# The thirty middle batches of a cross-attention kernel: code written out thirty times, or one body in a run-time loop

## The reference

```python
qn, kvn = layer_norm(q, g_q, b_q), layer_norm(kv, g_kv, b_kv)
Q, K, V = heads(qn @ Wq), heads(kvn @ Wk), heads(kvn @ Wv)      # 16 heads x 32
scores = einsum('bhqd,bhkd->bhqk', Q, K) / sqrt(32)
attn   = softmax(scores, axis=-1)
ctx    = einsum('bhqk,bhkd->bhqd', attn, V).reshape(B, N_q, 512)
out    = q + gelu(ctx @ Wo + bo)
```

## Time and profile before

| | |
|---|---|
| median of 3 runs | 3265.35 us (3262.8 to 3265.62) |
| the profiled execution's own time | 3262.8 us |
| its span, first to last instruction | 3261.0 us |
| PE busy | 3230.8 us, 99% of the span, 16611 matmuls |
| DVE, ACT, POOL busy | 69%, 70%, 71% |
| DMA | 343 MB, mean 105 GB/s |

### The profile page before, as it was taken

The page is one execution under the profiler, slowest core; times in us unless marked ns, Lnnn a source line. Parts: engine busy times, 40 slices in busy tenths (PEclk is TensorE's granted clock), DMA queues, the critical chain, the costliest instruction groups (busy, mean ns, idle before and its releaser), DMA issues.

```text
span 3261.0 us, 49855 instructions
## 1 busy us (share of the span) xinstructions
PE 3230.8 (99%) x16611; PEld 2135.1 (65%) x16611; DVE 2256.9 (69%) x4769; ACT 2280.3 (70%) x3985; POOL 2313.9 (71%) x1544
## 2 busy tenths in 40 slices
PE   8999999999999999999999999999999999999998
PEld 5566666666666666666666666666666666666664
DVE  6667667676676676666766766766667767667664
ACT  5677666777767777667767667776777676677765
POOL 3676776777677767777776677777767776777765
PEclk9999999999999999999999999999999999999999
DMA  5655656566556656565665566665656655666653
GB/s 142 87 108 107 108 104 116 91 111 107 107 104 104 111 107 107 104 118 89 111 109 106 105 102 111 109 104 104 120 86 112 107 107 107 100 111 108 105 79 76
DMA packets 186721, 343.02 MB, mean 105 GB/s; under 512 B 20561, under 2 KB 20577, under 8 KB 186466
## 3 DMA queue, kind: packets, MB, share of 16 engines
q1 hardware_dynamic: 186000, 339.03, 60.0%
q10 hardware_dynamic: 466, 0.80, 0.2%
HBM read 104.87 MB, written 33.55 MB: 42 GB/s over the span
## 4 chain that ended last, share of the span: by engine, by line
PE 97%; DVE 1%; ACT 1%; issue 1%; DMA 0%; POOL 0%; SPq 0%; ACTq 0%; POOLq 0%; DVEq 0%
PE gen L856 43%; PE score L883 16%; PE score L876 15%; PE ctx L903 14%; PE gen L847 4%; PE gen L943 4%; PE gen L965 1%; DVE maxes L706 1%; DMA k_stack<-k_nat 0%; ACT q_stack L617 0%; PE score L788 0%; ACT probs L563 0%; DVE stats L725 0%; PE gen L837 0%; POOL probs L475 0%
## 5 line engine op out<-in xcount | busy, mean ns | idle before, releaser
L475 POOL TENSOR_TENSOR probs<-probs 128x1024 f32<-128x1024 f32 x762 | 1800.3, 2392 | 287.8 <-PE ctx L903 281.6
L706 DVE TENSOR_REDUCE maxes<-score 128x1 f32<-128x512 f32 x2048 | 1294.9, 680 | 217.5 <-PE score L883 213.9
L563 ACT ACTIVATE probs<-score 128x512 f32<-128x512 f32 x2048 | 1090.2, 621 | 141.1 <-PE score L876 137.5
L883 PE MATMUL score<-k_stack,q_stack 96*128 96x512 f32 x2048 | 761.2, 413 | 3.3 <-DVE maxes L706 1.8
L876 PE MATMUL score<-q_stack,k_stack 128*128 128x512 f32 x2048 | 696.4, 406 | 6.6 <-ACT q_stack L617 6.5
L883 PEld LDWEIGHTS score<-k_stack,q_stack 96*128 96x128 f32 x2048 | 378.2, 188 | 221.3 <-ACT probs L563 83.6
L876 PEld LDWEIGHTS score<-q_stack,k_stack 128*128 128x128 f32 x2048 | 374.7, 188 | 199.9 <-DVE maxes L706 64.4
L903 PE MATMUL ctx<-probs,v_sb 128*32 128x512 f32 x4096 | 492.5, 598 | 0.0
L856 PE MATMUL gen<-cT,w_k 128*128 128x512 f32 x1536 | 461.7, 400 | 0.2 <-DVE q_nat L688 0.2
L856 PE MATMUL gen<-w_v,cT 128*128 128x512 f32 x1536 | 461.4, 395 | 0.0
L856 PE MATMUL gen<-xT,w_q 128*128 128x512 f32 x1536 | 447.9, 394 | 0.0
(11 more groups left out here) (89 smaller groups left out, 2765.4 us busy)
## 6 DMA issues: line engine op xcount, KB each, us to landing
k_stack<-k_nat SPq DMA_DIRECT2D x384, 256.0 KB, 7.6
q_stack<-q_nat SPq DMA_DIRECT2D x381, 256.0 KB, 5.6
tok<-in_x SPq DMA_DIRECT2D x132, 256.0 KB, 11.0
tok<-in_ctx SPq DMA_DIRECT2D x128, 256.0 KB, 12.0
res<-in_x SPq DMA_DIRECT2D x124, 256.0 KB, 2.7
out<-res SPq DMA_DIRECT2D x124, 256.0 KB, 2.1
probs<-in_L_xattn_Wq SPq DMA_DIRECT2D x1, 1024.0 KB, 8.2
probs<-in_L_xattn_Wk SPq DMA_DIRECT2D x1, 1024.0 KB, 10.4
```

The source lines that it names most:

```text
L475: pool.tensor_tensor(probs[:, c + 1, heads], probs[:, c + 1, heads], probs[:, c, heads], ALU.add).then_inc(pool_added, 1)
L563: act.activation(probs[:, n, part, :], score_at(s, "st", i)[:], ACT.Exp, scale=SCALE).then_inc(exp_done, 1)
L706: dve.tensor_reduce(maxes[:, u1 % 2, SROW + i:SROW + i + 1], score_at(s, "s", i)[:], AX_X, ALU.max, negate=True).then_inc(max_done, 1)
L883: pe.matmul(score_bank(pe, b, s, "s", i)[:, :], q_stack[0:KROWS, u1 % 2, n, P * part:P * (part + 1)], k_stack[0:KROWS, u1 % 2, n, :], star ...
```

## The change

`all_batches` is called once for each engine. The Python loop over the 30 middle batches, which wrote each batch's instructions out, becomes a loop that the engine executes: `eng.Fori(1, B - 1)` yields a value held in a register of that engine, and `batch(b)` is built once with it.

```diff
             batch(-1)
             batch(0)
-            for b in range(1, B - 1):
+            with eng.Fori(1, B - 1) as b:
                 batch(b)
             batch(B - 1)
             batch(B)
```

## The result

The changed kernel takes 3281.31 us, the median of 4 runs (3277.87 to 3283.67), against 3265.12 us (3262.8 to 3265.62, 4 runs) for the kernel before: a ratio of 1.0051, with a 95% interval of 1.0039 to 1.0063. It is slower by 16 us, where 161 us were forecast. What happened is rival 2, for which 3276 us had been worked out. (The profiled execution of the kernel before, 3262.8 us, is one of the runs counted, not a further one.)

A forecast was written before the change was run, and what follows sets the result against it. PE was taken as the bound, with no idle time to win. Jump stalls 107, lowered clock 49 and register instructions 4.5 made 161 us, giving 3426 us; the forecast's own range was 3390 to 3465, the stated range 3272 to 3462.

The forecast's parts named there:

- rival 2: PE's jump: the loop's beginning is still in PE's instruction memory; 3276 us, up to 3305; chance 0.21.
- What bounds the kernel: Middle batches: PE is busy 99% with no idle time to win; its sequencer's lead is nothing behind each step's transpose.
- I take it that the beginning must be fetched again, with PE waiting: PE's jump back: the body's first packet is refetched; PE idles 3.7 us at each of 29 jumps, 107 us.
- The price of a fetch: PE's jump: one fetch takes 3.5 us, 2.3 for the smallest load plus 1.2 for the packet; bounds 0 and 5.6.
- The clock after the stall: PE behind each jump: granted clock drops for 3.5 us, losing 1.7 us; 49 us over 29 jumps.
- The control instructions: PE's jump: register addition, branch and fused instruction add 0.2 us each time.
- Register instructions elsewhere: PE behind the three other transposes of a batch: one uncovered 51 ns instruction each, 4.5 us in all.
- The other engines' jumps: ACT, DVE, POOL, SP: fetches of 2.8 us are hidden, counted 0; 0.5 us per jump, 15 us, if cover is gone.
- the first: PE's jump: the fetch stalls PE but the clock does not fall; 3377 us, or 3342 with the lowest fetch; chance 0.15.
- The third: PE's jump: code is kept and the 0.2 us per jump is regained by earlier transposes; 3266 us, chance 0.12.
- The fourth: PE's body: kept code saves 4 fetches a batch, each costing 0.2 us unseen; faster, 3251 us, chance 0.05.

The follow-up runs named there:

- with the hint: Changed kernel with PE's loop body holding two batches, plus a compiler branch prefetch hint naming the back edge's target at the body's start: 3288.52 us, ratio 1.0082.

## Why the prediction was wrong

The measured time lies inside the range of 3272 to 3462 us only because the range was stretched to take in rival 2; the forecast itself, 3426 with 3390 to 3465, missed. (Those two ends are somewhat wider than a fetch of 2.5 to 4.5 us gives with the prediction's own terms, 3397 and 3455.)

- **What bounds the kernel** held: PE has nothing to win, and its sequencer has no lead behind the transpose. That the jump stands at such a place is the reason why it costs anything; eighteen matmuls later it costs nothing.
- **"I take it that the beginning must be fetched again, with PE waiting"** is the step that failed: 107 of the 161 us, and with them the 49 of the clock; the runs show no fetch at a jump, and 0.33 us in place of the 3.7 us of idle time. From the earlier trace rows it was right that packets come one at a time as the program is passed. It does not follow that what is passed is gone: a body of 1157 instructions is kept, with 13 packets in the whole run, and one of 2294 is not. The experiments with two batches to a pass show both sides. The profile before could not tell: a stream of new code fetches one packet per 256 instructions whatever the memory holds. That reason should have stopped me from giving this case 0.47.
- (The Trainium skill, "Runtime: NRT & Kernel Launch", section on instruction fetch mechanics, was used for the forecast with its two-page window. The runs decide against it: a jump back over 4.5 packets found its target. Its other number, 2048 instructions for PE, lies between the two bodies tried. Its 512 for the other engines do not say when a body is kept: 496 on ACT were not.)
- **The price of a fetch**, 3.5 us, was too low where there is one: 8.6 us, of which some 6 pass before the packet starts. I had taken the idle machine's load; the upper end that I named, 5.6 us, was passed as well.
- **The clock after the stall** went with the stall: it stayed 1.00. The step itself holds where the stall is made: PE's gaps of 8.5 to 8.8 us brought the lower level all 14 times, gaps of 3.2 to 3.8 us in 27 of 28 cases, those of 2.8 and 2.9 us (with the hint) not. But 2.9 to 6.1 us at the lower level behind the long stalls are more than the 3.5 that I took.
- **The control instructions**, 0.2 us, were 0.33 at each jump: 9.7 us in place of 5.8. The branch alone takes 0.21 us, where I had argued from a semaphore wait of 0.05. (The Trainium skill, "Advanced Engine Details and Errata", control flow timing, has 108 ns for a compare-and-branch. By their records PE's takes 208 ns and ACT's 45, and to the next instruction it is about 260 on both; neither agrees.)
- **Register instructions elsewhere**: 4.5 us forecast, 6.8 found, and at another place. I looked only behind the transposes on PE; the run with the late waits put back says that it comes from the wait that a register instruction carries on DVE and ACT, on the way from the transpose to the next `st`. An engine that is busy for 69% of its time can still be on PE's path at one instruction.
- **The other engines' jumps**, counted at 0, cost 0, as the run with PE written out shows. That holds for kept bodies: with 496 instructions on ACT it was 5.1 us per jump, where the prediction had at most 0.5 in mind. Its fetch of 2.8 us for these engines, which would have been hidden, was one of 7.2 to 7.5.
- **The rivals**: the first has the same fetch and falls with it. The second is the case. The third fails, as the 0.33 us are not regained. The fourth asked whether the fetches of before cost PE anything unseen: the trace of before, read around its packets, shows 4 ns for each, where 80 would have been needed.

## What to carry to other kernels

Before a loop is put in place of written-out code, count the instructions of its body on each engine; the question for the instruction memory is only whether the body is kept, and the packets of the instruction queues tell it at a glance. Then put the jump where the sequencer is ahead of its engine, which may be another place on each engine, and see that the wait that comes last rides on the instruction that works and not on a register instruction ahead of it. A stream of fetches in a profile without loops says nothing about what stays in memory.

## What the runs showed of the hardware beyond what was expected

- PE keeps a loop body of 1157 instructions and not one of 2294; ACT, DVE and POOL keep 251, 263 and 139, and ACT doesn't keep 496, nor DVE 521. Where between these it ends was not tried.
- A jump to code that is not kept holds PE's sequencer for 8.3 to 8.6 us in this kernel's traffic, and ACT's for 7.2 to 7.5; with the hint PE's branch took 0.36 us in the median.
- From the start of a taken branch to the first instruction of a kept body it is 266 ns on PE, 254 to 258 on ACT, POOL and SP, and 320 on DVE. The branch's own record, 208 ns on PE, 56 on DVE and 45 on the others, is not that time; on ACT it stays at 45 ns even where the code has to be fetched.
- A taken branch does not wait for the matmuls that are queued ahead of it: it was executed 2.9 us before PE had come to its place.
- On PE a register addition and a branch were not executed ahead of a matmul's unmet wait, though the wait rides on the matmul.
- A wait that comes last costs 0.03 to 0.04 us on the instruction itself and 0.12 us on a register instruction ahead of it (DVE, L771).
